# Cross-attention of a four-layer decoder: turning rounds on one row tile at a time beside score products of the next pair

## The reference, cut to what matters

```python
q_hk = (hidden_q @ Wq.T).reshape(B, S, 16, 128)
q_r = einsum(rope(einsum(q_hk, w_kc_q)), W_qr)      # 64 wide, per head
k_r = einsum(rope(kv_c), W_kr)
attn = softmax(einsum('bhsr,bhlr->bhsl', q_r, k_r))  # over 1500 positions
ctx_c = einsum('bhsl,bld->bhsd', attn, rope(kv_c))
return (einsum(ctx_c, w_kc_kv) reshaped) @ Wo.T
```

## Time and profile before

| | us |
|---|---|
| runs shown, median (lowest, highest) | 1676.99 (1670.87, 1678.79) |
| the profiled execution, its own time | 1670.51 |
| span of its instructions | 1668.7 |
| TensorE busy (matmuls) | 1624.9 |
| VectorE busy | 1112.9 |
| ScalarE busy | 748.2 |
| mean granted TensorE clock | 0.993 |

### The profile page before, as it was taken

The page is one execution under the profiler, slowest core; times in us unless marked ns, Lnnn a source line. Parts: engine busy times, 40 slices in busy tenths (PEclk is TensorE's granted clock), DMA queues, the critical chain, the costliest instruction groups (busy, mean ns, idle before and its releaser), DMA issues.

```text
span 1668.7 us, 35613 instructions
## 1 busy us (share of the span) xinstructions
PE 1624.9 (97%) x15226; PEld 1104.2 (66%) x15226; DVE 1112.9 (67%) x1964; ACT 748.2 (45%) x1288; POOL 239.3 (14%) x428
## 2 busy tenths in 40 slices
PE   8999999999999889999999999999999999999998
PEld 5575367777755656655367777764566767777765
DVE  2735899999566753266899999535445289999632
ACT  2213366666412641134366666312444366666411
POOL 0011200000010313011200000010455000000030
PEclk9999999999999999999999999999999999999999
DMA  9212020000040011051020000050300220000010
GB/s 279 73 26 82 1 77 2 2 2 2 2 187 1 2 59 40 1 118 63 1 96 2 2 2 2 2 241 1 64 1 1 114 89 2 2 2 2 2 45 11
DMA packets 35494, 71.10 MB, mean 43 GB/s; under 512 B 25331, under 2 KB 29747, under 8 KB 31405
## 3 DMA queue, kind: packets, MB, share of 16 engines
q1 hardware_dynamic: 35338, 68.83, 12.7%
HBM read 68.36 MB, written 0.46 MB: 41 GB/s over the span
## 4 chain that ended last, share of the span: by engine, by line
PE 90%; DVE 5%; ACT 2%; issue 1%; DMA 1%; POOL 1%; ACTq 0%; DVEq 0%; SPq 0%; POOLq 0%
PE ps L1106 14%; PE ps L1119 14%; PE ps L1019 13%; PE ps L351 10%; PE ps L1478 9%; PE ps L930 3%; PE ps L2549 3%; PE ps L1134 3%; PE ps L513 2%; PE ps L1918 2%; PE ps L940 1%; PE ps L2576 1%; PE ps L966 1%; PE ps L951 1%; PE ps L508 1%
## 5 line engine op out<-in xcount | busy, mean ns | idle before, releaser
L1220 ACT ACTIVATE arena<-ps,softmax_stats 128x1500 f32<-128x1500 f32 x168 | 254.0, 1512 | 192.8 <-DVE softmax_stats L1301 190.8
L1119 PEld LDWEIGHTS ps<-arena,ctx_pos 125*64 125x64 f32 x4608 | 222.3, 137 | 58.4 <-issue 55.4
L1106 PE MATMUL ps<-ident,arena 64*125 64x64 f32 x4032 | 239.2, 271 | 1.9 <-ACT arena L1220 1.6
L1119 PE MATMUL ps<-arena,ctx_pos 125*64 125x128 f32 (+1 forms) x4608 | 240.5, 262 | 0.0
L1106 PEld LDWEIGHTS ps<-ident,arena 64*125 64x125 f32 x4032 | 226.8, 185 | 17.0 <-issue 13.5
L1019 PE MATMUL ps<-ctx_feat,arena 64*128 64x500 f32 x1008 | 230.5, 590 | 0.0
L1227 ACT COPY arena<-ps 125x512 f32<-125x512 f32 x336 | 172.5, 599 | 77.8 <-PE ps L1106 77.8
L1299 DVE TENSOR_REDUCE softmax_stats<-ps 128x1 f32<-128x500 f32 x252 | 170.7, 678 | 48.9 <-PE ps L1019 48.5
L351 PE MATMUL ps<-arena 128*128 128x256 f32 x736 | 174.6, 383 | 2.9 <-ACT arena L2644 1.0
L1312 DVE TENSOR_SCALAR arena<-arena,softmax_stats 128x1500 f32<-128x1500 f32 x168 | 168.3, 1002 | 5.9
L1478 PE MATMUL ps<-x_feat,arena 128*128 128x448 f32 (+1 forms) x416 | 166.2, 544 | 1.2 <-DVE arena L1579 1.2
(11 more groups left out here) (319 smaller groups left out, 1923.4 us busy)
## 6 DMA issues: line engine op xcount, KB each, us to landing
ctx_pos<-in_ctx SPq DMA_DIRECT2D x1, 2688.0 KB
arena<-in_L1f_gate SPq DMA_DIRECT2D x1, 2304.0 KB, 12.0
arena<-in_L1f_up SPq DMA_DIRECT2D x1, 2304.0 KB, 17.0
arena<-in_L1f_down SPq DMA_DIRECT2D x1, 2304.0 KB, 7.8
arena<-in_L0a_Wq SPq DMA_DIRECT2D x1, 2048.0 KB, 10.5
arena<-in_L0a_Wc SPq DMA_DIRECT2D x1, 2048.0 KB, 19.4
arena<-in_L0x_Wq SPq DMA_DIRECT2D x1, 2048.0 KB, 10.1
arena<-in_L0x_Wo SPq DMA_DIRECT2D x1, 2048.0 KB, 8.4
```

The lines of the kernel that those rows point to most:

```text
L1106: m = nc.tensor.transpose(c.ps[0:LP, turn_bank(i, k, r), n * 64:(n + 1) * 64], probs[i % 2][e][rows, l * LP:(l + 1) * LP], c.ident[rows, r ...
L1119: m = nc.tensor.matmul(y[r * 64:(r + 1) * 64, lo:hi], c.ctx_pos[:, j, l, e, :], pT[i % 2][:, lo // 64:hi // 64, LT * e + l, :], start=(l = ...
L1220: nc.scalar.activation(probs[i % 2][e].rearrange("p (k l) -> p k l", k=3), sc[e], ACT.Exp, bias=low[:, i % 4, e:e + 1], accum_out=total[:, ...
```

## The change

For units 1 to 25 (`BESIDE`) the turning is written out anew, with the first score round (k = 0) of unit i + 2 inside it. Round 0 is turned on both row tiles as before. Then come: round 1 on row tile 0 alone; the score product of batch 1 on row tile 1; round 2 on row tile 0 alone; the score product of batch 0 on row tile 0; rounds 2 and 1 on row tile 1 alone. Before the product of batch 1 there is a wait for the exponential of batch 1 of the unit before (bank 3), before round 2 one for `kept`, before the product of batch 0 one for VectorE's copy (bank 0). The main loop leaves out the k = 0 scores where they were done so. The copy of round 0's second half goes from VectorE to ScalarE, which makes five copies a unit in the order (0,1), (1,0), (2,0), (2,1), (1,1); the counts waited for follow.

```diff
+    TURNED_BY_ACT = ((0, 1), (1, 0), (2, 0), (2, 1), (1, 1))
+    def third_free(i):
+        return 5 * i + (5 if i == 0 else 4)
...
-            if i > 1 and k < 2:
-                pe.wait_ge(d_in.handle, d_in.at(2 * (i - 2) + 1 + k))
+            if i > 1 and k == 0:
+                pe.wait_ge(d_in.handle, d_in.at(i - 1))
+            if i > 1 and k == 1:
+                pe.wait_ge(a_in.handle, a_in.at(5 * (i - 2) + 1))
             if i > 1 and k == 2:
-                pe.wait_ge(a_in.handle, a_in.at(4 * (i - 2) + 3))
+                pe.wait_ge(a_in.handle, a_in.at(third_free(i - 2)))
...
+        def turn_beside_scores(i):
+            turn(i, 0)
+            for n in range(8):
+                turn_block(i, 1, 0, n)
+            pe.wait_ge(exped[1].handle, exped[1].at(i + 2))
+            score_unit(i + 2, 0, 1)
+            pe.wait_ge(kept.handle, kept.at(i))
+            for n in range(8):
+                turn_block(i, 2, 0, n)
+            pe.wait_ge(d_in.handle, d_in.at(i + 1))
+            score_unit(i + 2, 0, 0)
+            for k in (2, 1):
+                for n in range(8):
+                    turn_block(i, k, 1, n)
+        BESIDE = range(1, NU - 2)
...
             for k in range(3):
-                score(i, k)
+                if k > 0 or i - 2 not in BESIDE:
+                    score(i, k)
...
-            for k in turn_order(i - 1):
-                turn(i - 1, k)
+            if i - 1 in BESIDE:
+                turn_beside_scores(i - 1)
+            else:
+                for k in turn_order(i - 1):
+                    turn(i - 1, k)
...
-                copy_turned(i - 1, 1, 0)
-                copy_turned(i - 1, 1, 1)
-                copy_turned(i - 1, 2, 1)
-                copy_turned(i - 1, 2, 0)
+                for k, r in TURNED_BY_ACT:
+                    copy_turned(i - 1, k, r)
...
-                copy_turned(i - 1, 0)
-                copy_turned(i - 1, 1)
+                copy_turned(i - 1)
```

More of the change, by code:

```diff
@@ L1003, in folded, with score_unit @@
             m.then_inc(*lat_mm.next())
+        def score_unit(i, k, e):
+            j, u = i // UNITS, i % UNITS
+            q = q2[:, j, :, :].rearrange("p h t -> p (h t)")[:, u * 128:(u + 1) * 128]
+            m = nc.tensor.matmul(sc[e][:, k, :], q[e * 64:(e + 1) * 64],
+                                 c.ctx_feat[e * 64:(e + 1) * 64, j, k * 4 * LP:(k + 1) * 4 * LP],
+                                 start=True, stop=True)
+            if e == 0:
+                m.then_inc(*scored[0].next())
+            elif k == score_order(i)[-1]:
+                m.then_inc(*scored[1].next())
         def score(i, k):
@@ L1011, in score @@
                     pe.wait_ge(exped[e].handle, exped[e].at(i))
[L1012 to L1013 removed]
+            if i > 1 and k == 0:
+                pe.wait_ge(d_in.handle, d_in.at(i - 1))
+            if i > 1 and k == 1:
+                pe.wait_ge(a_in.handle, a_in.at(5 * (i - 2) + 1))
             if i > 1 and k == 2:
[L1015 to L1017 removed]
+                pe.wait_ge(a_in.handle, a_in.at(third_free(i - 2)))
             for e in range(2):
[L1019 to L1025, removed]
+                score_unit(i, k, e)
         if rope:
@@ L1086, in _, with turn_block @@
         out_of_context(3)
+        def turn_block(i, k, r, n):
+            e, l = divmod(8 * k + n, LT)
+            rows = slice(r * 64, (r + 1) * 64)
+            m = nc.tensor.transpose(c.ps[0:LP, turn_bank(i, k, r), n * 64:(n + 1) * 64],
+                                    probs[i % 2][e][rows, l * LP:(l + 1) * LP], c.ident[rows, rows])
+            if n == 7:
+                m.then_inc(*(turned_hi if r else turned_lo).next())
         def turn(i, k):
@@ L1102, in turn @@
             for n in range(8):
-                e, l = divmod(8 * k + n, LT)
                 for r in range(2):
[L1105 to L1109, removed]
+                    turn_block(i, k, r, n)
+        def turn_beside_scores(i):
[13 more added lines that the diff above has]
+        BESIDE = range(1, NU - 2)
         def weigh(i):
             j, u = i // UNITS, i % UNITS
-            pe.wait_ge(a_in.handle, a_in.at(4 * (i + 1)))
-            pe.wait_ge(d_in.handle, d_in.at(2 * (i + 1)))
+            pe.wait_ge(a_in.handle, a_in.at(5 * (i + 1)))
+            pe.wait_ge(d_in.handle, d_in.at(i + 1))
             y = c.ps[:, 6, :]
@@ L1225, in copy_turned @@
             done = turned_hi if r else turned_lo
-            act.wait_ge(done.handle, done.at(3 * i + turn_order(i).index(k) + 1))
+            order = (0, 2, 1) if r and 1 <= i < NU - 2 else turn_order(i)
+            act.wait_ge(done.handle, done.at(3 * i + order.index(k) + 1))
             nc.scalar.copy(pT[i % 2][:, r, 8 * k:8 * k + 8, :],
```

12 lines of the change are left out of this document (6 added, 6 removed).

## The result

| | before | after |
|---|---|---|
| median of 4 runs each, us (lowest, highest) | 1677.89 (1670.87, 1679.0) | 1722.91 (1722.54, 1725.02) |
| ratio, 95% interval | | 1.029 [1.026, 1.032] |
| the profiled execution, us | 1670.51 | 1722.54 |

The change made the kernel 2.9% slower, as forecast; 1723 lies in the range, 18 us above the forecast of 1705. Profile against profile it is +52.0.

The account below looks back on a forecast made before the run. The prediction took TensorE, busy 97% and never still in a pass, as the bound. To the median of 1677 us it added 75 x 0.37 = 28 us of waiting for the second exponential, giving 1705; range 1688 to 1755.

Parts of the forecast that it names:

- (a): From first turning to the next pair's second score round, each row tile's work stays the same, 3.51 us.
- no overlap: Rival: a transpose never runs beside a product on the other tile; +2.61 us a pass, 1873 us, chance 0.05.
- (b): In the lone rounds, a transpose on one row tile takes a full step, 0.111 us.
- faster rival: Lone rounds turn at 0.056 us a transpose, so tile 1 ends 0.45 us early; 1643 us, chance 0.06.
- (d): Unlimited look-ahead: tile 1's product waits 0.74 us for the second exponential, 0.37 on the mean with tile 0's lead; 28 us.
- (c): How far TensorE looks past work stuck on one row tile: between one pending product and no limit.
- (e): Shallow look-ahead: tile 1's last two rounds enter behind 24 steps, 0.93 us a pass; 1747 us, chance 0.30 including in-between cases.
- near 1732: Look-ahead of four transposes: tile 1's last rounds enter 0.2 us earlier than shallow; shares the 0.30 chance.
- (f): Fifth copy moved to ScalarE: VectorE 6.8 us a pass, ScalarE 5.85; neither becomes the bound, no cost or gain.
- (g): New waits for copies have slack: 0.6 us at tile 0's score product, 0.4 before the third score round.
- deep: Case of (d), look-ahead limited by semaphores alone: a pass of 8.4 to 8.5 us, 1705 us, chance 0.48.

Follow-up runs that it names:

- e12_round: The changed kernel reordered: rounds 0 and 1 on both tiles, then each product beside a lone half of round 2, copies in round order; 1683.38 us, 1.008 of before.
- e6_runs8: The kernel before, only with the tiles taking turns within a turning round in runs of eight transposes instead of one; 1732.63 us, ratio 1.034.
- e7_runs4: The kernel before, only with the tiles taking turns within a turning round in runs of four transposes instead of one; 1671.57 us, ratio 0.998.
- e2_alone: The kernel before with the lone turning rounds but no score products between them, all scores in their old place; 1862.63 us, ratio 1.113.
- e3_mixed: The changed kernel with batch 1's product after four lone transposes and tile 1's round 2 mixed into tile 0's; 1703.98 us, 1.017 of before.
- e1_copy: The kernel before with only the copy of round 0's second half moved from VectorE to ScalarE; 1669.91 us, ratio 0.999.
- e11_late: The changed kernel reordered: 12 steps on both tiles before batch 1's product, the other transposes dealt out in groups of four; 1693.87 us, 1.012 of before.
- e10_split: The kernel before with 128-column transpose loads, the fifth copy on ScalarE, and round 2 split by tile around the second exponential's wait; 1617.94 us, ratio 0.966.
- e4_wide: The kernel before with transpose weight loads of 128 columns instead of 125, except each batch's last block; 1626.28 us, ratio 0.972.

## Why the prediction was right, and where its size was off

The sign and the mechanism hold: the work on each tile stays the same (a), nothing is gained, and tile 1 idles. By its steps:

- (a) and "no overlap": 3.52 us in e12_round for 3.51. A product beside transposes costs nothing. Holds.
- (b) 0.111 us a lone transpose: measured 0.109. Holds; the faster rival is out. (Its 3.06 had also left out the second exponential, which (d) lets the product start at 1.63 and not at 1.33; by (d) it would have been 3.37.)
- (c) left open between one product and no limit: it is three waiting records, shown by e6_runs8 and e7_runs4 on the kernel before, by e2_alone, and at two places of each pass of the trace after.
- (d) is the step that failed, as a size: it let an unlimited look-ahead set the time, so that only the second exponential cost anything. Its lead arrived (the exponential ended 0.38 earlier) and its price is about right where the order allows it (e3_mixed, +0.38 a pass; the release took 0.06 there and not 0.16). But in the change itself (c) comes later than (d): tile 1's rounds enter at 2.46 us, not at 2.19 as in e3_mixed. The likeliest case stood at 28 us; the trace has 55.6, of which e3_mixed keeps 30, and the other 25 are the limit's.
- (e) put those rounds at 2.67 (24 steps) and 0.93 a pass. It is 0.2 less, the "near 1732" case in between, 55 us: three waiting records of which two are the product's passes let tile 1 in with tile 0's seventh transpose. I gave all that lies between one common chance and forecast the other. The range held 1723 because it reached from the one case to the other, and the forecast came within 18 us of it partly by luck: the loops lost 55.6 us, the medians only 45.
- (f) holds (e1_copy); VectorE 6.95 and ScalarE 6.13 a pass for 6.8 and 5.9.
- (g) the slack held in the change: no wait of TensorE for a copy in its passes. It was thinner than it looked: the forecast took a transpose's completion to be told at once, and e11_late lost 0.17 and e12_round 0.2 a pass waiting for a copy.

My test "the first one-tile product starts 0.9 to 1.6 us after the turning (deep)" could not tell the cases apart: it started at 1.37 for the other reason. The place that tells them apart is the first transpose of tile 1 behind its product. And +0.74 without feedback, (d)'s upper figure, is the measured number by coincidence: e3_mixed has the feedback.

The Trainium skill, in "TensorE: Matmul & The Clock Gate", part 3, has matmuls start and end strictly in program order. The starts here do not (342.77 before three older ones), the completions seen by ScalarE in e3_mixed and e11_late do.

## What to carry to other kernels

Work for two row tiles must be mixed in the instruction stream at a grain of at most four records a tile: a longer run on one tile stops the other, though no profile row calls it a wait and the engine counts as busy. Before moving work between tiles, add up what each tile has to do: if neither has less afterwards and TensorE never stood still, the best result is a tie, and an added wait can only lose. (Where TensorE did stand, behind wide loads, dealing out one round anew gained 0.14 us a pass: e10_split.) A consumer of work on one tile also waits for older work on the other: ScalarE's copies came 0.4 to 0.5 us late by it in e3_mixed and e11_late.

## What the runs showed of the hardware

- At most three matmul records wait for a busy row tile; the fourth blocks the stream (in after, e2_alone and e6_runs8 what stood behind starts 6 ns after the first of four waiting ones does).
- A tile that ran dry needs 0.16 us to its second transpose, otherwise 0.11; in e6_runs8 six such starts a pass in place of one cost 0.28 us. A product's second pass follows its first after 0.52 us on such a tile (after), otherwise after 0.42 to 0.47.
- A transpose's completion is told only 0.05 us after an older product's pass on the other tile has ended (339.90 for 339.85 in e11_late, 309.26 for 309.21 in e3_mixed), though it ended itself 0.4 to 0.5 us earlier.
- On row tiles of 64 a transpose's weight load of 128 columns takes 138 ns (e4_wide), of 125 columns 186 (before). The score product's loads of 64x128 stay near 187 in both kernels.
- In e2_alone, whose lone transposes have nothing beside them, 44 of 75 passes were longer than the 9.5 to 9.6 of the others; one of 11.13 us shows a granted clock of 0.85.
